# Repeating the two broadcast matmuls of g in the first block and the tail of a state-space and experts kernel

## The chip, the cores and the metric

The kernel runs on one core of one Trainium2 chip. The metric is the device time of one execution in microseconds (us); lower is better.

## The reference, cut to what matters

```python
x = L0_attn_x                                    # (2, 1024, 256)
xn = layernorm(x)
# state-space part: D = 256 channels, N = 64 states, c_idx = t % 64
delta = softplus(delta @ dt_proj_w.T + dt_proj_b)
def step(h, inp):
    dt, b, xt, c = inp
    dA = exp(dt[:, :, None] * A)
    h = dA * h + dt[:, :, None] * b[:, None, :] * xt[:, :, None]
    y = einsum('bdn,bn->bd', h, c)
    return (h, y)
# experts part: 64 experts, 6 for each token, and one shared expert
out = x + (y + xn * D_param) @ out_proj_w.T + shared + routed
```

## The kernel before

**The scans.** The recurrence is computed as 256 scans on VectorE. One scan holds two channels of one batch on 128 partitions (2 channels x 64 states) and the 1024 steps of time along the free axis. The 256 scans are 8 blocks (`BLK`) of 32 (`SL`); a scan's number is `it * SL + s`. For scan c three inputs are made:

- the decay: TensorE broadcasts dt over the partitions into two PSUM banks (`bcast_dt`, two matmuls of 24 rows by 512 columns in bf16 against a selection matrix, banks 0 to 3 by turns), and ScalarE takes exp of the 1024 columns in place (line 867);
- g = dt * x, broadcast over the states in the same manner (`bcast_g`, matmuls through `spread`, line 1360);
- the product U = g * B. In the first block (scans 0 to 31) and in the tail (scans 219 to 255, `LATE = 219`) VectorE makes it itself in one piece of 1024 columns from the PSUM banks 4 and 5 (`two_g`, line 1188). In between, three of four products are made by GpSimd from rows that came by DMA or by a copy of ScalarE, and the fourth by VectorE in two halves of one bank each.

`two_g` is true for 32 + 37 = 69 scans. Each has one `bcast_g` of two matmuls, `spread(2, c, 4)` and `spread(3, c, 5)`. `spread(g, c, bank)` takes its 24 rows from partitions 32g on, so the two use different rows of the array.

**The order on each engine.** All is written out by hand. VectorE's body for scan s is scan(s), then product(s + 3). TensorE's body for step s is in the first block: `bcast_dt(s + 2)`, which waits for scan s; a part of the sums y over the states (`y_rows`, line 1349; in the first and last block 8 or 12 matmuls in each of seven steps of eight, `YSPREAD`); `bcast_g(s + 4)`, which waits by `g_used` for product(s + 3), because banks 4 and 5 have no second copy; and in the first 16 steps, at every second one, a step of the shared expert (`shared_step`, lines 1264 to 1276). In the tail the last of these is instead two or three rows of the experts' results added up in PSUM against a scaled identity (`add_row`, lines 1454 to 1459), each of which waits for a gather that GpSimd issues (line 724) and for a scaled identity that ScalarE makes (line 885). GpSimd scatters tokens in the first 27 steps (line 685). ScalarE's body takes `decay(s + 2)`, then the copies and activations of the experts.

The product of scan c waits for the semaphore `g_bcast`, which the second matmul of `bcast_g` raises by 2 when it is done. In the lines of the trace, line 1360 is any broadcast of dt or g (the helper `spread`), 1349 is y, 1188 the product, 1211 the scan.

Of the kernel before, what the change touches and what calls it, by code (L numbers as in the profile page):

```python
# [67 lines left out]
def state_space_and_experts(nc, x, xprojT, dtT, vecs, A_l, outT, gateT, gbias, w_up, w_down, w_exp, out):  # L68
# [5 lines left out]
    with ctx:  # L74
# [3 lines left out]
        def sem(name):  # L78
            return ctx.enter_context(nc.semaphore(name))
# [154 lines left out]
        g_bcast = sem("g_bcast")  # L234
# [63 lines left out]
        def by_vector(it, c):  # L298

            if isinstance(it, int):  # L300
                return sum(vector_tile(i) for i in range(it * SL + c))
            return NPRE + (it - PRE) * (SL // 4) + c // 4
# [7 lines left out]
        def by_act(it, c):  # L310

            if isinstance(it, int):
                return sum(not vector_tile(i) and i % 4 == 1 for i in range(it * SL + c))
            return (it - PRE) * (SL // 4) + (c + 2) // 4
# [13 lines left out]
        def two_g(it, c):  # L328

            return isinstance(it, int) and (it * SL + c < NPRE or it * SL + c >= LATE)  # L330
# [912 lines left out]
        def _(pe):  # L1243
# [35 lines left out]
            for n, (kind, q, _) in enumerate(JOBS):  # L1279
# [12 lines left out]
                if kind in ("xnT", "xn2T"):  # L1292
# [5 lines left out]
                    for j in range(4):  # L1298
                        ins = nc.tensor.transpose(bank[:, j * P:(j + 1) * P], src[:, 4 * g4 + j, h * P:(h + 1) * P],
                                                  ident[:, :])  # L1300
                elif kind == "logit":
                    if q == 0:
                        pe.wait_ge(act_evac, 8)
                    for j in range(8):
                        t = 8 * q + j
                        for k in range(2):
                            ins = mm(bank[:, j * 64:(j + 1) * 64], xnT[:, k, t * P:(t + 1) * P], Wgate[:, k, :],
                                     start=(k == 0), stop=(k == 1))
                elif kind in ("B", "C", "dpre"):
# [4 lines left out]
                    for k in range(2):  # L1314
                        if kind == "C":
                            ins = mm(bank[:, 0:PERIOD], Wproj[:, k, m0:m0 + P], xn2T[:, k, q * L:q * L + PERIOD],
                                     start=(k == 0), stop=(k == 1))
                        else:
                            ins = mm(bank, Wproj[:, k, m0:m0 + P], xn2T[:, k, 512 * q:512 * q + 512],
                                     start=(k == 0), stop=(k == 1))  # L1320
                elif kind == "dt":
                    h, tq = q // 4, q % 4
                    pe.wait_ge(act_evac, evac_no(JN["dpre", tq]))
                    ins = mm(bank, Wdt[:, h * P:(h + 1) * P], dpre[:, 512 * tq:512 * tq + 512], start=True, stop=True)
                else:
# [3 lines left out]
                    for k in range(TOPK):  # L1329
                        ins = mm(bank, ltri if q < 2 else onesb, OH[k][:, 512 * (q % 2):512 * (q % 2) + 512],  # L1330
                                 start=(k == 0), stop=(k == TOPK - 1))
# [21 lines left out]
            def parts_for(it, c):  # L1353

                q = c // SUB
                pe.wait_ge(s_pk[q % NPK], (it * (SL // SUB // NPK) + q // NPK + 1) * 16)

            def spread(g, c, bank):

                return mm(ps[:, bank, :], sel[32 * g:32 * g + ROWS, c % SUB, :],  # L1360
                          PK[32 * g:32 * g + ROWS, c // SUB % NPK, :], start=True, stop=True)
# [7 lines left out]
            def bcast_g(it, c, k):  # L1369
                v = by_vector(it, c)  # L1370
                parts_for(it, c)
                if two_g(it, c):
                    pe.wait_ge(g_used, 2 * v)
                    if it * SL + c >= LATE:
                        pe.wait_ge(moe_relu, NPAIR)
                        pe.wait_ge(g_copied, 2 * by_act(BLK, 0))
                    spread(2, c, 4)
                    spread(3, c, 5).then_inc(g_bcast, 2)
                else:
                    pe.wait_ge(g_used, 2 * v + k)  # L1380
                    spread(2 + k, c, 4).then_inc(g_bcast, 1)
# [10 lines left out]
            def body(it, moe):  # L1392
                for s in range(SL):
# [5 lines left out]
                    for k, c in ((1, s + 2), (0, s + GLEAD)):  # L1399
                        if not beyond(it, c) and half_g(it, c):  # L1400
                            if moe and pairs_until(n - 1):
                                pe.wait_ge(moe_relu, pairs_until(n - 1))
                            elif isinstance(it, int) and it == BLK - 1:
                                pe.wait_ge(moe_relu, NPAIR)
                            bcast_g(it, c, k)
# [28 lines left out]
                    if not beyond(it, s + GLEAD) and two_g(it, s + GLEAD):  # L1434
                        bcast_g(it, s + GLEAD, 0)
# [32 lines left out]

            pe.wait_ge(sel_turned, 1)
            bcast_g(0, 0, 0)  # L1470
            for c in range(DLEAD):
                bcast_dt(0, c)
# [65 lines left out]
```

## Time and profile before

| | |
|---|---|
| median of 3 runs | 994.73 us (993.2 to 996.29) |
| profiled execution, its own time | 987.29 us |
| its span, first to last instruction | 985.6 us |
| busy: PE, DVE, ACT, POOL | 813.2, 855.5, 589.6, 549.9 us |
| mean granted TensorE clock | 0.889 |

The span is in three parts that matter here: the first block (its scans start at 174 us), the blocks 1 to 6 and a part of block 7, and the tail (its products start at 788 us, the last scan ends at 960 us). PE is TensorE's matmuls, PEld its weight loads, DVE VectorE, ACT ScalarE, POOL GpSimd. A clock of 1.0 is 2.4 GHz and 0.5 is 1.2 GHz.

### The profile page before, as it was taken

How to read it: one execution, taken by the hardware profiler on the slowest of the kernel's cores; microseconds unless marked ns; L12 is line 12 of the kernel's file. 1: busy time of each engine (PE TensorE's matmuls, PEld its weight loads, DVE VectorE, ACT ScalarE, POOL GpSimd, SP SyncE). 2: the span in 40 equal slices, each digit the busy share in tenths (PEclk: the TensorE clock that was granted, in tenths of full speed). 3: DMA queues.
4: the chain of work that ended last, by engine and by line, in shares of the span. 5: the costliest groups of instructions: out<-in, count | busy, mean ns of one | idle time of the engine just before them, and what ended most of it. 6: DMA issues, size and time to landing. Idle time of an engine off the chain costs nothing.

```text
span 985.6 us, 19402 instructions
## 1 busy us (share of the span) xinstructions
PE 813.2 (83%) x6996; PEld 508.0 (52%) x6996; DVE 855.5 (87%) x690; ACT 589.6 (60%) x948; POOL 549.9 (56%) x372
## 2 busy tenths in 40 slices
PE   1967854687567999998999999899999678899888
PEld 1725532144124665665666665665665434445446
DVE  5699699987899899999999999999999967868852
ACT  3662126342245877887787887987887634444442
POOL 5000558655556666766666666667666745445540
PEclk9989896577557999999999999999999968897979
DMA  9649724622548899899899899899999522234324
GB/s 330 220 170 323 248 70 141 217 91 83 173 130 241 272 300 320 296 305 282 268 303 308 280 326 338 274 306 295 305 319 310 158 80 79 71 88 110 83 65 113
DMA packets 175983, 214.18 MB, mean 217 GB/s; under 512 B 49010, under 2 KB 135923, under 8 KB 175667
## 3 DMA queue, kind: packets, MB, share of 16 engines
q1 hardware_dynamic: 166674, 187.78, 59.9%
q0 software_dynamic: 9216, 25.18, 8.1%
q8 instruction: 58, 0.95, 0.4%
q14 instruction: 35, 0.28, 0.1%
HBM read 141.46 MB, written 71.30 MB: 216 GB/s over the span
## 4 chain that ended last, share of the span: by engine, by line
PE 52%; ACT 11%; DVE 10%; issue 6%; another core or an unknown queue 3%; SPq 1%; DMA 1%; DVEq 0%; ACTq 0%
PE ps L1349 20%; PE ps L1360 9%; PE ps L1466 6%; DVE H L1211 6%; PE ps L1419 6%; ACT ps L867 5%; PE ps L1457 4%; PE ps L1427 3%; DVE U L1188 3%; ACT YO L949 1%; PE ps L1454 1%; ACT GS L928 1%; ACT RL L916 1%; DMA WE<-w_exp_dram 1%
## 5 line engine op out<-in xcount | busy, mean ns | idle before, releaser
L1211 DVE TENSOR_TENSOR_SCAN H<-ps,U 128x1024 f32<-128x1024 f32 x256 | 581.1, 2283 | 29.4 <-ACT ps L867 26.2
L867 ACT ACTIVATE ps<-ps,Acur 128x1024 f32<-128x1024 f32 x256 | 279.0, 1090 | 214.2 <-PE ps L1360 169.7
L699 POOL TENSOR_TENSOR U<-X,B 128x1024 f32<-128x1024 f32 x94 | 223.5, 2379 | 142.0 <-DVE H L1211 125.6
L1349 PE MATMUL ps<-H,CB 128*32 128x128 f32 x4096 | 250.1, 395 | 4.7 <-issue 4.3
L1360 PE MATMUL ps<-PK,sel 24*128 24x512 bf16 x836 | 154.6, 423 | 98.7 <-DVE H L1211 51.1
L1349 PEld LDWEIGHTS ps<-H,CB 128*32 128x32 f32 x4096 | 138.7, 126 | 92.1 <-issue 41.3
L1360 PEld LDWEIGHTS ps<-PK,sel 24*128 24x128 bf16 x836 | 43.4, 92 | 213.3 <-issue 207.1
L685 POOL DMA_INDIRECT xg_d<-XN,slot x96 | 98.1, 1022 | 66.6 <-issue 28.1
L1188 DVE TENSOR_TENSOR U<-ps,B 128x1024 f32<-128x1024 f32 x69 | 83.3, 1207 | 54.2 <-remote 46.7
L699 POOL TENSOR_TENSOR U<-GS,B 128x1024 f32<-128x1024 f32 x47 | 112.7, 2397 | 30.4 <-DVE H L1211 27.2
L724 POOL DMA_INDIRECT WE<-yg_d,slot x66 | 62.4, 946 | 65.7 <-DVE H L1211 48.8
L1466 PE MATMUL ps<-WE,AS 128*128 128x256 f32 x320 | 92.2, 411 | 0.0
L1419 PEld LDWEIGHTS ps<-XT,WE 128*128 128x128 f32 x640 | 85.2, 195 | 6.5 <-issue 2.6
L1419 PE MATMUL ps<-XT,WE 128*128 128x128 f32 x640 | 86.9, 280 | 0.2 <-DMA WE<-w_exp_dram 0.2
L1466 PEld LDWEIGHTS ps<-WE,AS 128*128 128x128 f32 x320 | 55.0, 191 | 22.7 <-issue 18.3
L1193 DVE TENSOR_TENSOR U<-ps,B 128x512 f32<-128x512 f32 x92 | 61.2, 666 | 0.0
L733 POOL TENSOR_TENSOR U<-H,U 128x1024 f32<-128x1024 bf16 x6 | 12.6, 2137 | 85.2 <-DVE H L1118 85.2
L1427 PE MATMUL ps<-ident,XG 128*128 128x128 f32 x320 | 50.8, 282 | 10.7 <-ACT YO L949 10.7
L928 ACT COPY GS<-ps 128x512 f32<-128x512 f32 x94 | 56.3, 599 | 2.4 <-PE ps L1360 2.4
L923 ACT COPY XT<-ps 128x512 f32<-128x512 f32 x80 | 45.9, 574 | 6.2 <-PE ps L1427 5.0
L949 ACT COPY YO<-ps 128x512 f32<-128x512 f32 x80 | 47.4, 593 | 1.5 <-PE ps L1466 1.5
L1264 PE MATMUL ps<-xnT,WE 128*128 128x512 f32 x64 | 37.3, 738 | 8.0 <-issue 8.0
(196 smaller groups left out, 796.0 us busy)
## 6 DMA issues: line engine op xcount, KB each, us to landing
X<-g_d SPq DMA_DIRECT2D x94, 512.0 KB, 6.2
WE<-w_exp_dram SPq DMA_DIRECT2D x160, 256.0 KB, 4.2
xg_d<-CB SPq DMA_DIRECT2D x20, 1024.0 KB, 10.5
XG<-xg_d SPq DMA_DIRECT2D x80, 256.0 KB, 5.1
yg_d<-YO SPq DMA_DIRECT2D x80, 256.0 KB, 5.4
PK<-pk_d SPq DMA_DIRECT2D x64, 128.0 KB
pk_d<-H SPq DMA_DIRECT2D x12, 256.0 KB
X<-x_dram SPq DMA_DIRECT2D x4, 512.0 KB, 5.7
```

The source lines that it names most:

```text
L685: pool.indirect_dma_start(xg_d, bass.IndirectOffsetOnAxis(ap=slot[:, k, t:t + 1].bitcast(u32), axis=0), XN[:, t, :], None).then_inc(scatte ...
L699: nc.gpsimd.tensor_tensor(U[:, c % 4, :], rows, B2[:, b * L:(b + 1) * L], ALU.mult).then_inc(u_pool, 1)
L724: pool.indirect_dma_start(row(n), None, yg_d, bass.IndirectOffsetOnAxis(ap=slot[:, k, t:t + 1].bitcast(u32), axis=0))\
L867: nc.scalar.activation(a_tile(c), a_tile(c), ACT.Exp, scale=Acur[:, b, pair:pair + 1]).then_inc(a_ready, 1)
L928: nc.scalar.copy(GS[:, act_slot(c), 512 * k:512 * k + 512], ps[:, 5, :]).then_inc(g_copied, 1)
L1188: V.tensor_tensor(U[:, c % 4, :].rearrange("p (a c) -> p a c", a=2), ps[:, 4:6, :], B2[:, b * L:(b + 1) * L].rearrange("p (a c) -> p a c", ...
L1211: V.tensor_tensor_scan(H[:, (s // GRP % 2) * GRP + s % GRP, :], a_tile(s), U[:, s % 4, :], 0.0, ALU.mult, ALU.add).then_inc(scan_done, 1)
L1349: ins = mm(o, CB[:, b, 16 * j + i, :], hb[:, :, :, 16 * j + i], start=(i == 0), stop=(i == 15))
L1360: return mm(ps[:, bank, :], sel[32 * g:32 * g + ROWS, c % SUB, :], PK[32 * g:32 * g + ROWS, c // SUB % NPK, :], start=True, stop=True)
L1419: ins = mm(ps[:, 4, u * P:(u + 1) * P], W1[:, middle % MBUF, u, k, :], XT[:, u, k, :], start=(k == 0), stop=(k == 1))
L1427: ins = nc.tensor.transpose(ps[:, 6, k * P:(k + 1) * P], XG[:, taken % MBUF, k // 2, k % 2 * P:(k % 2 + 1) * P], ident[:, :])
L1466: ins = mm(ps[:, 6, u * D:(u + 1) * D], AS[:, u, :], W2[:, p % MBUF, u, :], start=True, stop=True)
```

## The change

In `bcast_g`, where both banks are filled at once, the pair of matmuls is issued three times. Each has `start=True`, so a later one overwrites an earlier one with the same values, and only the last raises the semaphore.

```diff
                     if it * SL + c >= LATE:
                         pe.wait_ge(moe_relu, NPAIR)
                         pe.wait_ge(g_copied, 2 * by_act(BLK, 0))
-                    spread(2, c, 4)
-                    spread(3, c, 5).then_inc(g_bcast, 2)
+                    for again in range(3):
+                        spread(2, c, 4)
+                        ins = spread(3, c, 5)
+                    ins.then_inc(g_bcast, 2)
                 else:
                     pe.wait_ge(g_used, 2 * v + k)
                     spread(2 + k, c, 4).then_inc(g_bcast, 1)
```

## Rows read from the trace of the kernel before

**Rows 1.** The page: busy time, and granted clock in tenths of 40 slices.
```profile
PE 813.2 (83%) x6996; PEld 508.0 (52%) x6996; DVE 855.5 (87%) x690; ACT 589.6 (60%) x948; POOL 549.9 (56%) x372
...
PEclk9989896577557999999999999999999968897979
```

**Rows 2.** Windows: length; busy PE, PEld, DVE, ACT, POOL; clock, DMA, GB/s.
```profile
169.00:201.00 32.00, 20.74 (x48) 6.24 (x49) 29.04 (x19) 10.67 (x13) 21.71 (x23) 0.55 0.65 219
201.00:236.00 35.00, 30.87 (x212) 17.47 (x211) 28.03 (x18) 10.59 (x13) 19.17 (x20) 0.79 0.22 76
236.00:286.00 50.00, 31.16 (x283) 13.18 (x285) 44.17 (x27) 15.60 (x17) 27.46 (x29) 0.53 0.55 172
788.00:958.00 170.00, 144.88 (x1012) 79.19 (x1012) 126.11 (x77) 71.92 (x140) 86.09 (x92) 0.82 0.30 84
```

**Rows 3.** Line 1188, the product, in the first block: ns, first and last start.
```profile
L1188 DVE TENSOR_TENSOR U<-ps,B x32: 1195/1198/1225, 168.8 to 284.2; 128x1024 f32<-128x1024 f32 x32
```

**Rows 4.** Line 1188 in the tail, and its idle time: releaser, us, times.
```profile
L1188 DVE TENSOR_TENSOR U<-ps,B x37: 1195/1198/1226, 788.0 to 946.8; 128x1024 f32<-128x1024 f32 x37
...
  remote: 36.0, 9
  PE ps L1360: 2.3, 3
```

**Rows 5.** Line 1188 from 236 to 286 us.
```profile
L1188 DVE TENSOR_TENSOR U<-ps,B x13: 1195/1198/1224, 239.6 to 284.2; 128x1024 f32<-128x1024 f32 x13
...
  remote: 3.3, 2
  PE ps L1360: 2.4, 3
```

**Rows 6.** Line 1360, the broadcasts, in the tail: ns, minimum, median, maximum.
```profile
L1360 PEld LDWEIGHTS ps<-PK,sel x148: 90/91/101, 788.2 to 953.3; 24*128 24x128 bf16 x148
L1360 PE MATMUL ps<-PK,sel x148: 371/385/604, 788.2 to 953.3; 24*128 24x512 bf16 x148
```

**Rows 7.** Timeline, a stretch of the tail at full clock.
```profile
910.45 2.28 DVE L1211 TENSOR_TENSOR_SCAN H<-ps,U 128x1024 f32<-128x1024 f32 x1
...
911.50 0.39 PE L1360 MATMUL ps<-PK,sel 24*128 24x512 bf16 x2
...
912.65 1.20 DVE L1188 TENSOR_TENSOR U<-ps,B 128x1024 f32<-128x1024 f32 x1
...
913.76 2.28 DVE L1211 TENSOR_TENSOR_SCAN H<-ps,U 128x1024 f32<-128x1024 f32 x1
...
915.26 1.70 PEld L1457 LDWEIGHTS ps<-WE,XT 128*128 128x128 f32 x8
915.48 1.89 PE L1457 MATMUL ps<-WE,XT 128*128 128x256 f32 x8
```

**Rows 8.** Timeline, two runs of line 1457 at half clock in the tail.
```profile
822.93 1.22 PE L1457 MATMUL ps<-WE,YO 128*128 128x256 f32 x2
...
840.44 2.07 PE L1457 MATMUL ps<-WE,YO 128*128 128x256 f32 x4
```

**Rows 9.** Timeline of the first block, scans 4 and 5, beside the shared expert.
```profile
188.52 0.61 PE L1360 MATMUL ps<-PK,sel 24*128 24x512 bf16 x4
...
189.55 1.20 DVE L1188 TENSOR_TENSOR U<-ps,B 128x1024 f32<-128x1024 f32 x1
```

**Rows 10.** Timeline of the first block after the shared expert's last step, half clock.
```profile
277.58 1.22 DVE L1188 TENSOR_TENSOR U<-ps,B 128x1024 f32<-128x1024 f32 x1 [0.35 <-PE ps L1360]
...
278.95 0.61 PE L1360 MATMUL ps<-PK,sel 24*128 24x512 bf16 x2
280.92 1.20 DVE L1188 TENSOR_TENSOR U<-ps,B 128x1024 f32<-128x1024 f32 x1
```

**Rows 11.** Timeline of a late product in the tail.
```profile
834.83 0.39 PE L1360 MATMUL ps<-PK,sel 24*128 24x512 bf16 x2
...
838.57 1.23 DVE L1188 TENSOR_TENSOR U<-ps,B 128x1024 f32<-128x1024 f32 x1 [3.81 <-remote]
```

## The prediction

> **What bounds the kernel now.** I read the page first: VectorE is busy for 87% of the span and TensorE for 83% [rows 1], an average over stages with different limits, so it does not tell what the change is worth. The line of tenths below shows where the granted clock of TensorE is not full: in the first block and in the tail, the two places where the change lies, and hardly between [rows 1]. So I cut the two places out as windows [rows 2], asked for the line of the product in each [rows 3, 4], and read the timeline for single steps [rows 7 to 11].
>
> The reader should see this. Where VectorE makes every product, it needs scan plus product for each scan, and where nothing is late the scans start 913.76 - 910.45 = 3.31 us apart [rows 7]. In the first block the 32 products start over 284.2 - 168.8 = 115.4 us, 3.72 us apiece [rows 3], and VectorE is idle for 117 - 29.04 - 28.03 - 44.17 = 15.8 us of the three windows [rows 2]. In the tail the 37 products take 946.8 - 788.0 = 158.8 us, 4.41 us apiece, with 36.0 + 2.3 = 38.3 us idle before 12 [rows 4]. VectorE therefore sets the pace in most steps, and in the tail it waits for g in 12 of 37. TensorE in the tail is busy 144.88 of 170 us at a clock of 0.82 [rows 2]. It is nearest to being the second bound.
>
> Some late products are not explained by what I can read. In [rows 11] the pair for g starts at 834.83 and would end at 835.2, yet the product starts only at 838.57 after 3.81 us idle, and until that product is done TensorE may not fill the banks again. I take these delays as given, neither longer nor more frequent after the change, and keep the doubt for the range.
>
> **The change, part by part.** Nothing is removed or moved, no DMA and no wait is added. Each of the 69 broadcasts of g gets four matmuls and their weight loads: 276 of each. All stand on TensorE between the wait for `g_used` and the signal `g_bcast`, so they delay the product of that scan, and everything behind them in TensorE's order: the next `bcast_dt`, hence ScalarE's exp, y, and the rows of the experts.
>
> *Price of one repeat.* A lone matmul of this form takes 385 ns by the median [rows 6], a pair of them 0.39 us [rows 7]: the two of a pair, on different rows of the array, run side by side. So a repeat costs the pitch of one matmul, not of two. No repeat on the same rows of the array is in the trace. The nearest rows are eight of the experts' matmuls in 1.89 us [rows 7]; with some 0.38 us for the last, seven pitches are 1.51 us, 0.216 each at full clock. At half clock four last 2.07 and two 1.22 us [rows 8], 0.425 each. I take these, since a lone one is as long as mine (0.38). Two repeats add 0.43 us at full clock and 0.85 at half. Lower bound: nothing, where the time is covered. Upper bound: no overlap between repeats, 0.385 plus a weight load of 0.09, 0.475 us, or 0.95 for two; at half clock 0.60 + 0.10, or 1.40 for two [rows 6].
>
> *First block, scans beside the up projection (169 to 201 us).* TensorE is busy 20.74 of 32 us at clock 0.55 [rows 2]. In [rows 9] the broadcasts start at 188.52, right behind the shared expert's matmuls, to end at 189.1; the product starts at 189.55. The margin is 0.4 us, the addition 0.85, so each of the four steps that have such work before them comes 0.45 us later: **2 us**. The steps between have room.
>
> *Beside the down projection (201 to 236 us).* TensorE is busy 30.87 of 35 us at 0.79 [rows 2], so 0.42 of the time is at half clock and two repeats cost 0.58 x 0.43 + 0.42 x 0.85 = 0.61 us. For the nine products of that stretch 5.5 us; a third may fall into the gaps: **4 us**.
>
> *After the shared expert (236 to 286 us).* Busy 31.16 of 50 us at 0.53 [rows 2]: room enough, but the signal's own path counts. Where 8 matmuls of y stand before g, g starts at 278.95, ends at 279.6, and the product starts at 280.92: 1.3 us of margin cover the 0.85. Where 12 stand before it, the product waits already (0.35 us, [rows 10]). Five of the 13 products there are late now, by 3.3 + 2.4 = 5.7 us [rows 5]; each becomes later by 0.85: **4 us**. What covers the other eight is the scan that VectorE does meanwhile, with TensorE idle 38% of the stretch; without that cover they would cost 6.8 us more.
>
> *Tail.* At 0.82 the share at half clock is 0.36, and two repeats cost 0.64 x 0.43 + 0.36 x 0.85 = 0.58 us; 37 of them are 21.5 us of TensorE's time. The 12 late products [rows 4] take it in full: 7 us. In the 25 others there is a margin: the pair at 911.50 ends at 911.89 and its product starts at 912.65 [rows 7], so 0.76 us covers 0.43. But the repeats also push the rest of the order, and TensorE is busy 85% of this stretch; the 15% it is idle lies largely behind late products, as that of [rows 11], where the repeats cannot go, since they stand behind the same wait. I let a third of 0.58 come through, 0.2 us, for 25 products: 5 us. Together **12 us**. If nothing came through it would be 7, if all did 21.5.
>
> Sum: 2 + 4 + 4 + 12 = 22 us. The profiled execution took 987.29 us, so 1009.3, 2.2% more. The median of the runs shown is 994.73, higher by 0.75%; by the same ratio it becomes 1017 us.
>
> **A rule against the trace.** In [rows 7] eight weight loads (1.70 us) lie inside the eight matmuls (1.89 us) that use the whole array: a load ran while the matmul before it still did. The Trainium skill ("TensorE: Matmul & The Clock Gate", Part 3, The mechanism) says of matmuls on parts of the array that a weight load overlaps matmuls in flight only when its row group differs; it names the background weight buffer as another way. Here each repeat loads the same row group as the one before it. By that rule repeats would not overlap, and the time would be that of the first rival below; the rows on the whole array do not agree with it.
>
> **The rivals.**
>
> *Repeats in series.* If a repeat must wait for the one before, two cost 0.95 and 1.40 us. Then the four steps beside the up projection lose 1.0 each (4 us), the nine beside the down projection two thirds of 0.58 x 0.95 + 0.42 x 1.40 = 1.14 (7 us), the later stretch 5 x 1.40 and 8 times the 0.1 by which 1.40 passes the margin of 1.3 (8 us), the tail 12 x 1.11 and, with TensorE behind in most steps, about 0.7 for 25 (31 us): 50 us, 1037 us by the profile, 1045 by the median. For it: nothing in the trace has two matmuls of a broadcast on the same rows back to back. Against it: the loads in [rows 7]. It decides from a pitch of 0.47 us.
>
> *Covered.* VectorE sets the pace in 25 of the tail's 37 steps and in most of the first block, with margins of 0.4 to 1.3 us; and the late products may be late for something that the repeats run beside. Then only a few tenths per block are left: 987 to 990 us by the profile, 995 to 998 by the median. Against it: [rows 10] has a product that waits for exactly this pair.
>
> *A warmer clock, faster than before.* TensorE is at 1.2 GHz almost throughout 236 to 286 us, where it is busy 62% of the time, and at 2.4 GHz in the blocks between, where it has little idle time [rows 1, 2]. The repeats lift the 62%: 13 x 0.85 = 11 us more of 50, to 84%. If the clock then stays full there, the waits of that stretch (5.7 us, [rows 5]) fall away, and if it comes to full sooner in the tail, about a fifth of the 38.3 us: 5.7 + 7.7 = 13.4 us gained. The repeats at full clock still cost 0.43 in some 17 steps, the 12 late products of the tail and five beside the down projection, 7 us: 980 to 981 us by the profile, 988 by the median. It decides from the point where the stretch 236 to 286 us shows a clock near 1.0. Against it: at 201 to 236 us TensorE is 88% busy and has only 0.79; the slow phases of the tail follow late products, where TensorE issues nothing and the repeats stand behind the wait; and most of the stretch is VectorE's pace anyway. The Trainium skill ("TensorE: Matmul & The Clock Gate", Part 1, What's actually happening) has the same mechanism: the throttled state is the default and activity releases it. The trace agrees in kind, 0.53 beside 62% busy.
>
> **How the numbers follow.** A measurement of this kernel tells about 0.3%, 3 us, from no change. Chances: the forecast 0.64 (its own range 1004 to 1030, from 7 us in the tail and part of the first block to all 21.5 with the late products somewhat later still), repeats in series 0.10, covered 0.14, warmer clock 0.12. So faster 0.12, same 0.14, slower 0.74. The range reaches from 991, which takes in the covered case, to 1040, between the forecast's upper end and the series case; about 2 in 10 is outside, half on either side.
>
> **What would show it.** In the changed kernel's trace: six matmuls of a broadcast with a pitch of 0.22 us between pairs at full clock and 0.43 at half (series: 0.47 or more); 3.31 us between most scans still; the products of the first block over about 125 us rather than 115.4, those of the tail over about 171 rather than 158.8; the middle blocks unchanged. More than 12 late products in the tail, and later ones, would say that I underrated how the repeats push TensorE's order. The prediction is wrong if the clock of 236 to 286 us rises to near 1.0 and the products there come at 3.31 us each, or if the long delays of [rows 11] change in number, for I do not know what makes them.

## The result

The changed kernel takes 1002.77 us by the median of 20 runs (992.52 to 1010.11), the kernel before 995.5 us (20 runs, 987.24 to 1002.04): a ratio of 1.0065, 95% interval 1.0042 to 1.0087. It is slower, as forecast, by 6.5 us instead of 22. The forecast of 1017 us was too high by 14; the range, 991 to 1040, held the time. Runs more than 1.5% above the fastest of their kernel count as slow and are left out of all ratios; the profiles of the pair five times in the tail and of the tail part once more are of such runs, and are left out of the means below.

The profiled execution of the changed kernel took 1003.45 us, its span is 1001.7 us. That of before took 987.29 us, 8 us less than its median, so the two profiles lie 16 us apart where the medians lie 7: one pair of profiles does not measure the change. The page of the changed kernel, busy time and clock, beside [rows 1]:

```profile
PE 841.1 (84%) x7271; PEld 514.1 (51%) x7272; DVE 856.3 (85%) x690; ACT 590.4 (59%) x948; POOL 550.5 (55%) x372
...
PEclk9989886679557898999999999999999867899999
```

The windows of [rows 2] in the changed kernel:

```profile
169.00:201.00 32.00, 21.09 (x70) 6.05 (x70) 25.55 (x17) 8.26 (x10) 19.24 (x21) 0.61 0.60 206
201.00:236.00 35.00, 30.74 (x217) 15.82 (x220) 26.87 (x17) 11.54 (x15) 19.22 (x20) 0.84 0.24 84
236.00:286.00 50.00, 39.02 (x317) 15.31 (x306) 41.62 (x26) 14.74 (x17) 28.13 (x30) 0.61 0.48 153
788.00:958.00 170.00, 145.69 (x1123) 73.86 (x1121) 128.86 (x77) 71.06 (x135) 86.62 (x87) 0.86 0.29 80
```

TensorE is busier after the shared expert (39.02 of 50 us instead of 31.16) and its clock there is 0.61, not near 1.0. In the tail the clock rose from 0.82 to 0.86.

The line of the product, in the first block and in the tail, beside [rows 3, 4]:

```profile
L1188 DVE TENSOR_TENSOR U<-ps,B x32: 1199/1212/1226, 169.4 to 292.1; 128x1024 f32<-128x1024 f32 x32
...
L1188 DVE TENSOR_TENSOR U<-ps,B x37: 1199/1224/1226, 799.9 to 964.1; 128x1024 f32<-128x1024 f32 x37
...
  PE ps L1360: 21.3, 6
  remote: 21.2, 7
```

The products of the first block take 122.7 us (115.4 before), those of the tail 164.2 (158.8 before). The forecast was 125 and 171.

The price of a repeat shows in the timeline: the six matmuls of one broadcast at half clock in the first block, and at full clock in the tail.

```profile
270.08 1.46 PE L1360 MATMUL ps<-PK,sel 24*128 24x512 bf16 x6
...
271.65 1.23 DVE L1188 TENSOR_TENSOR U<-ps,B 128x1024 f32<-128x1024 f32 x1
...
883.36 0.82 PE L1360 MATMUL ps<-PK,sel 24*128 24x512 bf16 x6
...
885.37 1.23 DVE L1188 TENSOR_TENSOR U<-ps,B 128x1024 f32<-128x1024 f32 x1 [3.74 <-PE ps L1360]
```

A pair lasts 0.61 and 0.39 us, so two repeats add 1.46 - 0.61 = 0.85 us at half clock and 0.82 - 0.39 = 0.43 at full, as forecast to the hundredth. Repeats do not run in series. In the first two lines the product starts 0.11 us after the six end. The last two lines are a long delay: the six end at 884.2, the product starts only 1.2 us later, at 885.4, after 3.74 us of idle time. In the kernel before, the product of the same scan (236) idles almost as long, with its pair done 3.0 us ahead of it:

```profile
864.90 0.39 PE L1360 MATMUL ps<-PK,sel 24*128 24x512 bf16 x2
...
868.28 1.22 DVE L1188 TENSOR_TENSOR U<-ps,B 128x1024 f32<-128x1024 f32 x1 [3.65 <-remote]
```

The pair comes later in the changed kernel, and the product hardly does.

### The profile page after: what moved, and what is told of

Same layout as the page of the kernel before. It is cut to its first block, busy times and chain, and to the rows that moved or that the text cites. A ratio compares the mean times of both kernels' runs of the same rounds, so it can differ in the third digit from the quotient of the medians.

```text
span 1001.7 us, 19953 instructions
## 1 busy us (share of the span) xinstructions
PE 841.1 (84%) x7271; PEld 514.1 (51%) x7272; DVE 856.3 (85%) x690; ACT 590.4 (59%) x948; POOL 550.5 (55%) x372
## 4 chain that ended last, share of the span: by engine, by line
PE 54%; DVE 11%; ACT 10%; issue 6%; another core or an unknown queue 2%; POOL 0%; DVEq 0%; ACTq 0%; POOLq 0%
PE ps L1349 20%; PE ps L1360 11%; DVE H L1211 8%; PE ps L1468 7%; PE ps L1421 6%; ACT ps L867 5%; PE ps L1459 4%; PE ps L1429 3%; DVE U L1188 2%; ACT YO L949 1%; PE ps L1456 1%; ACT GS L928 1%; PE ps L1270 1%; ACT RL L916 1%
## 5 line engine op out<-in xcount | busy, mean ns | idle before, releaser
L1360 PE MATMUL ps<-PK,sel 24*128 24x512 bf16 x1112 | 189.0, 433 | 84.9 <-DVE H L1211 40.3
L1360 PEld LDWEIGHTS ps<-PK,sel 24*128 24x128 bf16 x1112 | 52.0, 96 | 215.6 <-issue 204.9
L699 POOL TENSOR_TENSOR U<-GS,B 128x1024 f32<-128x1024 f32 x47 | 112.6, 2395 | 30.8 <-DVE H L1211 27.6
L1429 PE MATMUL ps<-ident,XG 128*128 128x128 f32 x320 | 52.0, 287 | 10.7 <-ACT YO L949 10.7
L733 POOL TENSOR_TENSOR U<-H,U 128x1024 f32<-128x1024 bf16 x6 | 12.6, 2133 | 85.8 <-DVE H L1118 85.8
L1429 PEld LDWEIGHTS ps<-ident,XG 128*128 128x128 f32 x320 | 35.7, 146 | 17.8 <-issue 15.8
```

Of the source, the lines that this page charges most:

```text
L699: nc.gpsimd.tensor_tensor(U[:, c % 4, :], rows, B2[:, b * L:(b + 1) * L], ALU.mult).then_inc(u_pool, 1)
L1429: ins = nc.tensor.transpose(ps[:, 6, k * P:(k + 1) * P], XG[:, taken % MBUF, k // 2, k % 2 * P:(k % 2 + 1) * P], ident[:, :])
```

## The experiments

All ratios are to the kernel before on the same chip, with their 95% interval. A run's "products" are the time from the first to the last start of the product's line in a place, as in [rows 3, 4].

### One place at a time, and the dose

The number of times that the pair is issued becomes a constant for each place. This is the edit for the first block alone, against the changed kernel; for the tail alone 1 and 3 are exchanged, and the higher doses have 5 or 7 in place of 3:

```diff
-                    for again in range(3):
+                    for again in range(3 if it * SL + c < NPRE else 1):
```

> The pair is issued three times in the first block only, once in the tail. Theory A (the forecast: the repeats come through in both places): this half costs 10 us, 1.0% over before. Theory B (in the profiles the products of the first block take 122.7 us instead of 115.4, those of the tail's scans no more than before, so the cost is in the first block): 5 to 8 us, nearly all of the change's 0.65%. Theory C (what is seen is spread over both and the tail's share is hidden by chance in one profile): 3 us.

Measured: 1.0092 (1.0057 to 1.0127), 9 us, with an interval of 6 to 13: near theory A's 10, and theory B's 5 to 8 is inside too. Theory C's 3 us falls. Products of the first block 126.8 us, of the tail 159.8.

> The pair is issued three times in the tail only. Theory A: 12 us, 1.2% over before. Theory B: within 2 us of before, because a margin of some 0.7 us ahead of most products covers 0.43 us and the long delays swallow the rest. Theory C: 3 to 4 us. A fourth, D: the repeats keep the clock up in the tail (0.86 instead of 0.82 in the profiles) and this pays for them; then the clock of the tail is higher here than in the run that has them in the first block only.

Measured: 1.002 (0.9987 to 1.0053), 2 us, at most 5. Theory A's 12 us falls. The clock from 788 to 958 us is not higher than in the run above (0.80 here, 0.81 there), so theory D falls. Theory B stands, with most of the cost in the first block; theory C's 3 to 4 us for the tail can't be told from its 2.

> The pair is issued seven times in the first block, six repeats instead of two: 1.28 us more at full clock and 2.55 at half. Theory A, proportional: 30 us. Theory B (margins of 1.1 to 1.3 us in the later stretch are used up, and TensorE has more work in a step than VectorE): more than three times the cost of two repeats, 25 to 45 us, unless the clock goes to full from 236 us on, when 1.28 us fit into the margins and the cost stays near 15 us.

Measured: 1.0386 (1.0326 to 1.0447), 38 us; products of the first block 158.9 us. From 236 to 300 us TensorE is busy 58.28 of 64 us, and the clock is still only 0.67. The interval is 32 to 44: above theory A's 30 us, within theory B's 25 to 45. Six repeats cost about four times what two do, but the intervals allow three times as well. VectorE waits for the six repeats before 28 of the 32 products (53.8 us), where in the kernel before it waits for the pair before 6 (5.0 us); that the margins are used up is my reading of this.

> The pair is issued seven times in the tail: 1.28 us more at full clock for each of 37 products. Theory A, proportional to 12 us for two repeats: 36 us. Theory B (a margin of some 0.7 us): 25 products x (1.28 - 0.76) = 13 us, and the late ones up to 12 x 1.28 = 15 more, 13 to 28 us. Theory D: the clock in the tail is at 0.95 or more, and the cost is under 15 us.

Measured: 1.0176 (1.0114 to 1.0237), 17.5 us, within theory B's 13 to 28. The clock in the tail's window is 0.90. Theory A's 36 us falls, and so does theory D.

> The pair is issued five times in the tail: 0.86 us more at full clock, 1.7 at half. A margin of about 0.7 us that covers the first 0.43: a knee, so the cost lies below the middle of that of two repeats (2 us) and six (17 us): 5 to 9 us. Cost proportional to the repeats once TensorE's load counts: 10 us or more.

Measured: 1.0142 (1.0075 to 1.0209) by four runs, 14 us, with an interval of 7.5 to 21. That is above the 5 to 9 us of a knee, whose upper end the interval only just takes in. A straight line from nothing to 17.5 us at six repeats has 6 us at two and 12 at four, where 2 to 4 and 14 were measured: a bend between two and four is likely, and not shown.

### The same load on another path

The pair of dt in place of the pair of g, first block only.

```diff
-                spread(0, c, 2 * (c % 2))
-                spread(1, c, 2 * (c % 2) + 1).then_inc(dt_bcast, 1)
+                for again in range(3 if isinstance(it, int) and it * SL + c < NPRE else 1):
+                    spread(0, c, 2 * (c % 2))
+                    ins = spread(1, c, 2 * (c % 2) + 1)
+                ins.then_inc(dt_bcast, 1)
```

> In the first block the pair of dt, not that of g, is issued three times: the same matmuls in the same number, on the path to ScalarE's exp instead of the path to the product. Theory I (in the first block the cost is that of the signal's path: g may start only after a product and must be there for the next): these repeats fall into TensorE's wait for the product and cost 0 to 3 us. Theory J (the cost is TensorE's load): 6 to 9 us, as with g.

Measured: 1.0046 (1.0009 to 1.0084), 4.6 us: between the two theories, with an interval of 1 to 8 us that takes in both. The products of the first block take 124.6 us in its profile, as long as with g's repeats, which speaks for TensorE's load (theory J). It decides nothing.

### Where the tail's late products come from

Gathers of the tail as plain DMAs of SyncE, under the same waits. The edit is shown by its core; the loop around it moves to SyncE with it. In this and all later kernels with plain gathers or scatters the rows come and go in their stored order, and what is left out is the reading of the experts' slots: the experts' part of the output is then that of other tokens.

```diff
-                pool.indirect_dma_start(row(n), None, yg_d,
-                                        bass.IndirectOffsetOnAxis(ap=slot[:, k, t:t + 1].bitcast(u32), axis=0))\
-                    .then_inc(s_g[n % RING], 16)
+                sp.dma_start(row(n), yg_d[n * P:(n + 1) * P, :]).then_inc(s_g[n % RING], 16)
```

> No repeats. The 96 indirect gathers of the tail, which GpSimd issues, are replaced by plain DMAs of 128 rows each from SyncE's queue, at the same steps and under the same waits; they bring rows in their stored order, so the experts' part of the output is that of other tokens. Theory E (the long delays of products in the tail, 3 to 10 us each and 11 to 13 of them, come with GpSimd's indirect DMAs): they are gone in the tail, scans 216 to 255 take about 130 to 140 us instead of 172, and the time falls by 30 to 40 us. Rival F (they come from TensorE's own order, whatever brings the rows): the same number of late steps, within 5 us of before.

Measured: 0.9549 (0.9494 to 0.9603), 42 us less. The product's line in the tail, whose number is 1196 there (columns as in [rows 4]):

```profile
L1196 DVE TENSOR_TENSOR U<-ps,B x37: 1199/1199/1226, 796.3 to 917.6; 128x1024 f32<-128x1024 f32 x37
its engine sat idle before it (us, times) until:
  PE ps L1368: 1.6, 3
```

121.3 us instead of 158.8, 1.6 us idle instead of 38.3. That is VectorE's pace: 36 steps of 3.31 us are 119.2. The long delays of this stretch come with the indirect gathers.

> As the run with plain DMAs, and the pair is issued three times in the tail. Read against that run. Theory G (in the change the long delays swallow the repeats, so that without them each of 37 comes through): 12 to 20 us slower than it. Theory H (the margin ahead of the product covers them in any case): within 4 us of it.

Measured: 0.9651 (0.9598 to 0.9703). Against the run before it, 0.9651 / 0.9549 = 1.011, 8 us between the medians (949.6 and 957.78), in the profiles more:

```profile
L1196 DVE TENSOR_TENSOR U<-ps,B x37: 1199/1225/1225, 787.3 to 919.9; 128x1024 f32<-128x1024 f32 x37
its engine sat idle before it (us, times) until:
  PE ps L1368: 10.7, 12
```

132.6 us, 11.3 more than without repeats, 12 late products with 10.7 us of idle time. Theory G stands: with the long delays away, the repeats come through, and nearly to the size of the forecast's 12 us.

The same with the gathers left on GpSimd, but in the plain form, `pool.dma_start(row(n), yg_d[n * P:(n + 1) * P, :])`:

> No repeats. The tail's gathers stay on GpSimd and keep its order and waits, but are plain DMAs of 128 rows. If the long delays come with DMAs whose descriptors GpSimd writes, whatever their form, the tail keeps 10 or more late steps and the time is within 8 us of before. If they come with the indirect form (the scattered reads of rows) only, the tail takes 130 to 140 us and the time falls by 30 to 40 us.

Measured: 0.9564 (0.9521 to 0.9607). The gathers and the product's line in this run:

```profile
L724 POOL DMA_DIRECT2D WE<-yg_d x66: 536/536/616, 785.0 to 919.8; - x66
...
L1186 DVE TENSOR_TENSOR U<-ps,B x37: 1199/1199/1226, 787.4 to 910.2; 128x1024 f32<-128x1024 f32 x37
its engine sat idle before it (us, times) until:
  PE ps L1358: 2.4, 3
```

The same engine issues 96 DMAs at the same steps (66 of them in this line) and the delays are gone. It is the indirect form, not GpSimd's DMAs as such. The indirect ones also take their rows from scattered places, the plain ones in order; no run has the indirect form with rows in order, so these two are not told apart. In the kernel before an indirect one takes 946 ns on GpSimd, a plain one here 536.

> All gathers plain but issued by GpSimd, and the pair of g is issued three times in the tail. Read against the run with GpSimd's plain gathers. If the absence of the delays exposes the repeats: 8 to 12 us slower. If it was SyncE's queue: within 3 us.

Measured: 1.0107 (1.0081 to 1.0134) to the kernel before on its chip, of which more below. The line of the product:

```profile
L1186 DVE TENSOR_TENSOR U<-ps,B x37: 1197/1224/1227, 778.4 to 913.8; 128x1024 f32<-128x1024 f32 x37
its engine sat idle before it (us, times) until:
  PE ps L1358: 13.4, 13
```

135.4 us, 12.6 more than the 122.8 without repeats on the other chip, with idle time of 13.4 instead of 2.4 us: it was not SyncE's queue that exposed the repeats.

The scatters of the first block as plain DMAs of SyncE too, `sp.dma_start(xg_d[n * P:(n + 1) * P, :], XN[:, t, :])`, without and with the repeats there:

> No repeats. The tail's gathers as plain DMAs of SyncE, and the 96 scatters of the first block as plain DMAs of SyncE as well (in stored order, so the experts work on other tokens). Theory E for the first block too (its late products come with GpSimd's indirect DMAs): scans 0 to 29 take 97 to 103 us instead of 111 to 118, and the time falls by another 10 to 16 us against the run with plain gathers only. Rival: the late steps of the first block come from TensorE's own work at half clock, and they stay within 4 us.

Measured: 0.9427 (0.9388 to 0.9467), 54 us less than before. Products of the first block, line 1202:

```profile
L1202 DVE TENSOR_TENSOR U<-ps,B x32: 1199/1199/1226, 168.0 to 272.8; 128x1024 f32<-128x1024 f32 x32
its engine sat idle before it (us, times) until:
  PE ps L1374: 6.0, 4
```

104.8 us instead of 115.4, and 13.4 us less than with plain gathers (from GpSimd) alone on this chip (947.04 and 933.61). Most of the late products of the first block come with the indirect scatters. Form and engine changed together here, so that it is the form is taken over from the gathers.

> As the run with all DMAs plain, and the pair is issued three times in the first block. Read against that run: if the long delays cover repeats in the first block as they do in the tail, 10 to 14 us slower than it; if they cover none there, the same 6 to 9 us as with the indirect scatters.

Measured: 0.9492 (0.9449 to 0.9535), 1.007 of the run above, 6 us. Products of the first block:

```profile
L1202 DVE TENSOR_TENSOR U<-ps,B x32: 1199/1214/1225, 168.2 to 277.1; 128x1024 f32<-128x1024 f32 x32
its engine sat idle before it (us, times) until:
  PE ps L1374: 9.2, 8
```

4.1 us more. No cover shows in the first block, where the repeats cost 4 to 6 us without delays and 9 (6 to 13) with them.

### A chip on which the delays do not occur

Every second gather plain, the others indirect, without and with repeats in the tail; then both limits of two DMAs in flight. These three and the run of plain gathers with repeats ran on one chip, another than the runs above.

```diff
+                if n % 2:
+                    pool.dma_start(row(n), yg_d[n * P:(n + 1) * P, :]).then_inc(s_g[n % RING], 16)
+                    return
                 pool.indirect_dma_start(row(n), None, yg_d,
```

> No repeats. Of the tail's gathers, all issued by GpSimd, every second one is a plain DMA, the others stay indirect. If each indirect DMA has its part in the long delays: about half of what the tail loses to them (43 us in the profile of before) comes back, scans 216 to 255 take 145 to 155 us, and the time falls by 15 to 25 us. If the delays need indirect DMAs back to back, nearly all of it, 35 to 40 us.

Measured: 0.9992 (0.9973 to 1.0011), no change, which neither theory had. The reason is the kernel before: on this chip it takes 935.76 us by the median of 17 runs (932.23 to 940.32), where the other chips gave 987 to 996. The profile of this run, with all 96 scatters and 48 of the gathers indirect:

```profile
L727 POOL DMA_INDIRECT WE<-yg_d,slot x33: 971/976/1021, 772.9 to 905.8; - x33
...
L1191 DVE TENSOR_TENSOR U<-ps,B x32: 1193/1198/1226, 168.7 to 272.0; 128x1024 f32<-128x1024 f32 x32
...
L1191 DVE TENSOR_TENSOR U<-ps,B x37: 1187/1191/1226, 775.0 to 896.4; 128x1024 f32<-128x1024 f32 x37
its engine sat idle before it (us, times) until:
  PE ps L1363: 1.6, 3
```

103.3 and 121.4 us: no long delay, with the indirect form in place. So the delays need the indirect form and depend on the chip: three of the four chips on record had them, one had not. The kernel before has no profile on that chip; its 936 us are those of the kernel with all DMAs plain on another (933.61).

> As the run with every second gather plain, and the pair of g is issued three times in the tail. Read against that run. If the long delays are what covers the repeats (2 us with all of them, 8 to 12 without), a cost between, 4 to 8 us. If the plain DMAs of SyncE, not the absence of the delays, had exposed the repeats: 2 us.

Measured: 1.0104 (1.0069 to 1.014), against the run above 945.83 - 934.98 = 10.9 us; products of the tail 131.0 us, 9.6 more. It does not test a part cover, since nothing was there to cover, but shows once more what the repeats cost without delays. A late product of it:

```profile
856.83 0.82 PE L1363 MATMUL ps<-PK,sel 24*128 24x512 bf16 x6
...
858.12 1.23 DVE L1191 TENSOR_TENSOR U<-ps,B 128x1024 f32<-128x1024 f32 x1 [0.92 <-PE ps L1363]
```

The last of the six ends at 857.65, when VectorE has been idle for 0.45 us, and the product starts 0.47 us later.

### Fewer indirect DMAs in flight

A gather waits until the one two before has landed; nothing is left out.

```diff
+                if n >= 2:
+                    pool.wait_ge(s_g[(n - 2) % RING], 16 * ((n - 2) // RING + 1))
                 pool.indirect_dma_start(row(n), None, yg_d,
```

> No repeats. A gather of the tail waits until the one two before it has landed, so at most two are in flight. If the long delays come from many of GpSimd's DMAs in flight at once, fewer of them and a time 10 to 30 us below before; if each of the 96 instructions has its part in them, the same or slower, because the waits stretch the gathers.

Measured: 0.9899 (0.9856 to 0.9943), 979.97 us against 987.18 of before on its chip, 7 us by the medians and 10 (6 to 14) by the ratio: on a chip with the delays it is faster than before, where the change was slower in both of its comparisons. Products of the tail 143.7 us instead of 158.8, though what follows the end of the last scan grows from 25.3 to 32.9 us, as I take it because the rows come late.

> No repeats. Both the gathers of the tail and the scatters of the first block wait until the one two before has landed. If the delays of the first block shrink as those of the tail did: 3 to 8 us below the run that limits the gathers only, 15 us below before. If not, equal to it.

Measured, on the chip without delays: 1.0575 (1.0549 to 1.0602), 54 us slower. The limit on the scatters holds up GpSimd's products behind them: VectorE waits once for 21.0 us for the first of them. And the limit on the gathers costs there too: products of the tail 145.0 us where that chip needs 121. So the limit is a gain only where the delays are. In this profile, and but for one product at 0.91 us in the one before it, no product of the tail starts more than 0.5 us after its pair: what idle time the limit leaves (23.7 and 22.0 us) is TensorE coming late with the pair.

### The change and its tail part, once more

> The change itself, once more, beside before on the same chip. In the last four runs before took 936 us on their chip, 50 us less than on the two chips used until then, and their profiles show no long delays though half or all of the indirect DMAs are in. If this chip is of that sort (before near 936): the repeats are exposed, 12 to 20 us slower, 1.3 to 2.1%. If it is of the other sort (before near 990): 4 to 9 us slower, as first measured.

Measured: 1.0129 (1.0082 to 1.0176), 13 us, beside a kernel before at 986.93 us, a chip with the delays; 4 to 9 us were expected there. Its products take 120.1 us in the first block and 161.7 in the tail.

> The pair three times in the tail only, once more. On a chip without the long delays (before near 936): 8 to 12 us slower, 0.9 to 1.3%. On a chip with them: 0 to 4 us, as first measured.

Measured: 1.0044 (1.0013 to 1.0075), 4 us. With the first comparison's 1.002 the tail's part is 0.3%, 3 us, where the delays are. The two parts add up to 11 to 13 us, the change itself measured 6.5 and 13: the second agrees and the first, with the most runs, does not. On which chip the first was measured is not on record; the gap stays open.

## Why the prediction was right and wrong

**Price of one repeat: right.** 0.85 and 0.43 us are what the six matmuls show. I had the pitch from matmuls of another form (128 rows, f32, 256 columns); that it would hold for mine was an assumption until then. The rival of repeats in series, and with it the rule about row groups, did not hold: in the changed kernel the weight loads of the repeats run beside the matmuls before them, and three pairs last 0.82 us where the series would take 0.39 + 0.95 = 1.34. The Trainium skill's sentence ("TensorE: Matmul & The Clock Gate", Part 3, The mechanism) names the background buffer as the other way. The trace agrees that loads of the same row group can overlap (0.82 us for three pairs); whether that buffer does it no run here shows.

**First block, 2 + 4 + 4 = 10 us: the sum about right, its parts not.** Alone it measured 9 us. The products of the first block took 122.7, 126.8 and 120.1 us in the three kernels with these repeats and the delays, and 113.4 to 120.7 in seven profiles without (115.4, 114.1, 120.7, 120.3, 116.4, 113.8, 113.4: mean 116.3), 7 us more by the means (123.2). By the starts of single products the first ten take 3.4 us more (36.2 against 32.8, forecast 2), the next nine 1.6 (39.9 against 38.3, forecast 4), the last thirteen 1.8 (47.1 against 45.2, forecast 4). Single profiles scatter by 1 to 6 us in these parts, but as far as the means tell the two later terms measured under half of their forecast and the first more than its own: that the sum is near is in part luck. Left out of my working was the start: the first three products stand one behind the other with no scan between to cover their broadcasts. The first scan starts at 176.5, 176.0 and 176.0 us in the three, and at 173.2 to 174.8 in those without: 2 us.

**Tail, 12 us: the step that failed.** Measured 2 and 4 us where 12 were forecast. The sum 12 x 0.58 + 25 x 0.2 took two things for independent: it let the 12 late products "take it in full", and it took the delays as a fixed addition. In a kernel or on a chip without the delays the 12 us are nearly right: 11.3, 12.6 and 9.6 us in three pairs of profiles (the second pair across two chips), 8 to 11 us by the medians of the two pairs within one chip, 12 or 13 late products. With the delays 3 us: products of the tail 158.8, 159.8, 163.8 and 160.6 us without repeats there (mean 160.8), 164.2, 161.7 and 166.0 with them (mean 164.0). So the long delays swallow some 8 of 11 us. That they do so is shown: three pairs without the delays, and two runs of the tail's part with them (2 and 4 us). A fourth profile with them, of a slow run, has 167.5 us, which would make it 4 us instead of 3.

How they do it can be read from the time between the end of a pair (or of the last repeat) and the start of its product, for the products before which VectorE stood idle. In the tails without delays, on whatever chip, it is 0.1 to 0.5 us. In each of the ten profiles with all gathers indirect, no limit and the delays it is more, 0.7 to 6.0 us, for 7 to 10 products: the pair is done by the profile, and what tells VectorE of it has not come. The profile's ends of matmuls are modelled, so whether the matmuls or their signals are late it does not say. Added up, what this time exceeds 0.1 us by in those products is 31.8, 27.9, 30.8 and 32.6 us in the four tails without repeats and 24.3, 15.8 and 23.0 in the three with them, 10 us less by the means. So the pairs end later by about what the repeats cost, and VectorE is released when it would have been anyway. Single steps show the same: the step from scan 222 takes 7.58, 7.76 and 7.71 us in before, in the change and with the tail's repeats alone, that from scan 233 7.06, 7.16 and 7.11, while the pair for the product in that last step (scan 236) ends 3.0, 1.2 and 0.85 us ahead of it. In the first block this sum shrinks as well (from 20.3 to 10.5 us by the means), and the repeats cost their price there all the same; why it differs stays open.

**The warmer clock: wrong as a cause of the time.** With two repeats the clock from 236 to 286 us went from 0.53 to 0.61 with TensorE busy 78% of it, and with six to 0.72, busy 91% (45.25 of 50 us); nothing was gained. In the tail the clock is 0.86, 0.80 and 0.83 in three profiles with the same repeats and 0.82 and 0.81 in two without, so the rise to 0.86 does not repeat: no pay-back to be seen.

**Covered:** I gave it 0.14 for the whole change. It was right for the tail, and for the reason that it named, that the late products are late for something beside which the repeats run; it was wrong for the first block. The doubt stated with [rows 11] was the place to look: of the 38.3 us idle in the tail 36 to 37 go with those delays (1.6 to 2.4 us remain without them), and I put a price on top of each without knowing what ended it.

**What would show it:** the pitch of 0.22 and 0.43 us: right. First block 125 us: 122.7. Tail 171: 164.2. The middle blocks, whose code is the same, take 495.4 us from scan 29 to 214 before and 499.4 after: 4 us that I can't put to a step of the change, and within the 494.5 to 501.2 of the other runs, with and without repeats (the limit on the scatters aside, which has 515.6).

## What to carry to other kernels

A late consumer is no proof that work ahead of it will be paid in full: find out what ends the wait first. Where the profile shows the producer done and the consumer still waiting, more work for the producer may cost nothing, and the same work costs its full price as soon as that wait is cured, so an edit measured beside a stall has to be measured again without it. And a margin that exists in one step (0.76 us at [rows 7]) says little of a stretch in which an engine is busy 85%: the dose (two, four, six repeats: 2 to 4, 14 and 17.5 us) does.

## What the runs showed of the hardware

Indirect DMAs issued by GpSimd go with late releases: for 7 to 10 products of the tail 0.7 to 6.0 us pass between the end of TensorE's matmuls and the start of VectorE's product, where otherwise 0.1 to 0.5 us do, though the DMAs share no data with those matmuls. They cost 42 us of 992 in the tail, and with the scatters of the first block 54 of 987. The plain form has none, the gathers' from GpSimd or from SyncE, the scatters' from SyncE. On one chip of four the same indirect scatters and half of the gathers had none either, and the kernel before, with all of them indirect, took 936 us instead of 987 to 996. At most two gathers in flight took the tail's products from 158.8 to 143.7 us. What in the chip makes the delays, and what sets the fourth chip apart, stays open. So does what the change costs there, where it was not run; an estimate from its parts is 15 to 17 us, 1.6 to 1.8%: 10.9 us for the tail on that chip, 4 to 6 us for the first block with all DMAs plain on another.
